# Two transformer layers on one core: queries, keys and attention outputs turned by DMA through DRAM instead of on TensorE, and layer 0's raw scores in blocks of 32 queries

## The reference

```python
# layer 0: 16 query heads and 4 key/value heads of 16 channels, rotary embedding, window of +-64 tokens
q, k = rope(x @ wq), rope(x @ wk); v = x @ wv
att = softmax(where(|i - j| <= 64, q k^T * 16 ** -0.5 + sink, -inf)); x = ln(x + (att @ v) @ wo)
x = ln(x + qmatmul(silu(qmatmul(x, w_gate)) * qmatmul(x, w_up), w_down))      # int8 weights, 1024 wide
# layer 1: 16 heads, causal, bias; then top 2 of 16 experts and a shared one
q, k, v = split(x @ w_qkv.T + b_qkv); q, k = rope(q), rope(k)
x = ln(x + (softmax(causal(q k^T / 4)) @ v) @ w_out.T + b_out)
x = ln(x + shared(x) + sum over the 2 chosen experts of weight * expert(x))
```

## Time and profile before

| | us |
|---|---|
| median of 3 runs | 926.04 (922.36 to 928.40) |
| the profiled execution | 922.61 |
| its span | 920.8 |
| PE busy, share | 772.8, 84% |
| DVE busy, share | 572.9, 62% |
| ACT busy, share | 456.1, 50% |
| POOL busy, share | 402.1, 44% |
| moved by DMA | 43.21 MB, 47 GB/s on average |

### The profile page before, as it was taken

One profiled execution on the slowest core, in us unless ns is written; L12 is line 12 of the kernel. 1 busy time (PEld: TensorE's weight loads), 2 busy tenths in 40 slices (PEclk: granted clock), 3 DMA queues, 4 the chain that ended last, 5 costly groups with the idle time before them and its releaser, 6 DMA issues.

```text
span 920.8 us, 15561 instructions
## 1 busy us (share of the span) xinstructions
PE 772.8 (84%) x5309; PEld 612.3 (66%) x5309; DVE 572.9 (62%) x1421; ACT 456.1 (50%) x990; POOL 402.1 (44%) x698
## 2 busy tenths in 40 slices
PE   5668888888878699977989999999978688899955
PEld 3567776766656577866756667766745566789845
DVE  4677776666523445457666677687741558699923
ACT  2226654555544344344455566667644243467503
POOL 4457655544455355566132234227155260145521
PEclk8879997999969899999699999999996589799978
DMA  8700000000000000000000000001045520245452
GB/s 227 178 1 1 2 2 1 1 2 2 2 1 1 0 1 1 1 1 1 2 1 1 2 2 1 3 1 48 1 165 186 122 91 9 81 139 156 138 207 92
DMA packets 26724, 43.21 MB, mean 47 GB/s; under 512 B 5972, under 2 KB 20054, under 8 KB 25784
## 3 DMA queue, kind: packets, MB, share of 16 engines
q0 software_dynamic: 6688, 23.30, 8.2%
q1 hardware_dynamic: 17248, 16.19, 6.3%
q10 hardware_dynamic: 2712, 2.73, 0.9%
HBM read 20.31 MB, written 14.60 MB: 38 GB/s over the span
## 4 chain that ended last, share of the span: by engine, by line
PE 65%; DVE 15%; POOL 8%; ACT 4%; issue 4%; DMA 2%; ACTq 0%; DVEq 0%; SPq 0%; POOLq 0%
PE ps L1726 9%; PE ps L1862 7%; PE ps L1880 7%; PE ps L1849 7%; PE ps L2287 4%; PE ps L2010 4%; DVE negmax L1310 3%; PE ps L1755 3%; PE ps L2027 3%; PE ps L2304 2%; PE ps L1842 2%; POOL fT L752 2%; PE ps L1764 2%; PE ps L2200 2%; PE ps L1845 2%
## 5 line engine op out<-in xcount | busy, mean ns | idle before, releaser
L1310 DVE TENSOR_REDUCE negmax<-ps 128x2 fp32r<-128x512 f32 (+4 forms) x304 | 189.6, 631 | 128.8 <-PE ps L1849 124.1
L941 ACT ACTIVATE prob<-ps 128x448 f32<-128x448 f32 (+2 forms) x320 | 168.8, 532 | 184.2 <-PE ps L1862 182.3
L1862 PE MATMUL ps<-qT,kT 128*128 128x256 f32 (+4 forms) x512 | 138.1, 337 | 42.9 <-DVE kT L1302 24.1
L1849 PE MATMUL ps<-kT,qT 128*128 128x256 f32 (+4 forms) x512 | 163.5, 389 | 0.0
L1862 PEld LDWEIGHTS ps<-qT,kT 128*128 128x128 f32 x512 | 87.8, 201 | 64.5 <-issue 51.3
L705 POOL TENSOR_SCALAR_AFFINE_SELECT prob<-prob 128x512 f32<-128x512 f32 (+1 forms) x192 | 115.8, 629 | 0.0
L1849 PEld LDWEIGHTS ps<-kT,qT 128*128 128x128 f32 x512 | 101.2, 212 | 2.6
L700 POOL TENSOR_TENSOR carry_p<-neg_half 128x1 f32<-128x1 f32 x80 | 16.7, 208 | 177.5 <-ACT prob L941 177.4
L1880 PE MATMUL ps<-prob,v_aug 128*32 128x256 f32 (+4 forms) x1024 | 84.8, 444 | 3.2 <-POOL prob L705 3.2
L836 POOL DMA_INDIRECT token_y<-ys_sb,y_row x47 | 45.0, 958 | 75.9 <-DVE ys_sb L1680 75.3
L1726 PE MATMUL ps<-wqkv_s,xh 128*128 128x384 f32 (+2 forms) x288 | 62.3, 354 | 10.1 <-DVE xh L1239 10.0
(11 more groups left out here) (237 smaller groups left out, 1673.0 us busy)
## 6 DMA issues: line engine op xcount, KB each, us to landing
xs_sb<-slot_x SPq DMA_DIRECT2D x47, 129.0 KB, 2.1
w_sb<-in_w POOLq DMA_DIRECT2D x4, 1408.0 KB, 12.0
w_sb<-in_w POOLq DMA_DIRECT2D x4, 704.0 KB, 9.6
x_all<-in_x SPq DMA_DIRECT2D x4, 512.0 KB, 9.4
slot_x<-zeros SPq DMA_DIRECT2D x1, 2048.0 KB, 22.6
w_sb<-token_y SPq DMA_DIRECT2D x2, 1024.0 KB, 10.4
w_sb<-token_y ACTq DMA_DIRECT2D x2, 1024.0 KB, 11.4
out<-y_all SPq DMA_DIRECT2D x4, 512.0 KB, 2.8
```

What stands on the lines that cost most here:

```text
L941: act.activation(prob[l][:, part % PROB_BUFS, i % GH, 0:cols], ps[:, 2 + n % 2, 0:cols], ACT.Exp, scale=SCALE).then_inc(exped[l].sem, 1)
L1310: dve.tensor_reduce(out=negmax[:, g % 2, t, j * mh:(j + 1) * mh], in_=ps[:, k % 2, 0:mh * n].rearrange("p (h n) -> p h n", n=n), axis=AX.X ...
L1849: ins = pe.matmul(dst[:, jj, :], qT[l][g % RING][:, h // 2, t * P:(t + 1) * P], kT[l][g % RING][:, h if l == 1 else h % 2, k0:k0 + n], sta ...
L1862: ins = pe.matmul(ps[:, 2 + item % 2, col:col + n], kT[l][g % RING][:, h if l == 1 else h % 2, kt * P:(kt + 1) * P], qT[l][g % RING][:, h ...
```

## The change

- **Queries and keys.** The projection is now made with the weights at rest and 512 tokens moving (`block_of`, L1901), so that it comes out transposed: 3 blocks for a batch in layer 0, 4 in layer 1 (there the values stay apart, `v_product1`). ACT copies a block to `raw_sb`, SP swaps the halves of each rotary pair by DMA (`swap`), POOL multiplies with the cosines, DVE with the sines and adds (`rope`), ACT and POOL make the high and the low part. SP writes both to DRAM (`write`) and reads them back for each group, already stacked as 48 rows for a head (`read`). `turn_q`, `turn_k`, the stacks and the copies of `qT` and `kT` are gone.
- **Attention outputs.** `oT` is written to DRAM and read back as numerators and denominators (`o_write`, `o_read_in`). For every two groups, in slot 4 of each odd step from 5 on, DVE takes the reciprocal of 512 columns and multiplies 512 (`divide`), then subtracts the high part (`o_low`). `o_transposes`, `o_turn` and the division of 16 columns are gone; the output products come one step later.
- **Raw scores of layer 0.** They go by blocks of 32 queries with 96, 128 or 160 keys. The four heads of the group lie beside each other on four column groups of PE, the operands are read as plain float32, and a group has 6 items, of 8, 8, 12, 12, 12 and 12 matmuls; four column groups of 32 are how `pv_part` too is laid out, before and after. The maxima are spread by one DVE operation and turned by one matmul.
- **Order.** In layer 1 the blocks of one batch instead of two are made in the feed-forward stage. Zeros for `slot_x`, 2 MB, are written after layer 0's steps instead of at the start; the later weights and inputs, 2.3 MB, stand behind the first group's read; the experts' first weights come at step 12 instead of 15, the shared ones after the scores.

What SP issues is now an ordered stream in which each entry waits for its own data, and all behind it wait with it.

```diff
-            def turn_q(l, g, n, bank):
-                pe.wait_ge(*q_lo[l].ge(g + 1))
-                for t in range(NT):
-                    ins = pe.matmul(ps[:, bank, t * P:(t + 1) * P],
-                                    q_st[l][g % Q_STACKS[l]][:, t, 2 * n:2 * n + 2, :].rearrange("p h s -> p (h s)"), ident_r[:],
-                                    start=True, stop=True)
-                ins.then_inc(q_tr[l].sem, 1)
...
+            def block_of(l, n, bank):
+                b, k = divmod(n, N_KINDS[l])
+                c0 = BLOCK_COLS[l][KINDS[l][k]]
+                pe.wait_ge(*xh_lo[l].ge(NT // 2 * (b + 1)))
+                for i, (a, w_part) in enumerate(EXACT):
+                    for k in range(KC):
+                        ins = pe.matmul(ps[:, bank, :], wqkv_s[l][:, w_part, k, c0:c0 + P], xh[:, a, k, :],
+                                        start=(i + k == 0), stop=(i == 2 and k == KC - 1))
+                ins.then_inc(blk[l].sem, 1)
...
+            def rope(l, n):
...
+                sines = rot[0:rows, 1, :] if rows == P else rot_k[0:rows, :]
+                dve.tensor_tensor(out=swap_sb[0:rows, n % 2, :], in0=swap_sb[0:rows, n % 2, :], in1=sines,
+                                  op=ALU.mult).then_inc(sined[l].sem, 1)
+                dve.wait_ge(*sined[l].ge(n + 1))
+                dve.wait_ge(*cosd[l].ge(n + 1))
+                dve.tensor_tensor(out=rope_sb[0:rows, n % 2, :], in0=rope_sb[0:rows, n % 2, :], in1=swap_sb[0:rows, n % 2, :],
+                                  op=ALU.add).then_inc(roped[l].sem, 1)
...
+            def write(l, n):
+                b, k = divmod(n, N_KINDS[l])
+                kind, rows = KINDS[l][k], rows_of(l, n)
+                m = 0 if kind == "kv" else int(kind[1])
+                dst, hi_at, lo_at = (q_dram, slice(0, 2), 2) if kind[0] == "q" else (k_dram, slice(0, 3, 2), 1)
+                sp.wait_ge(*hi_put[l].ge(n + 1))
+                sp.dma_start(dst[l][b, m, hi_at, :, :].rearrange("r p t -> p r t"),
+                             hi_sb[0:rows, n % 2, :].bitcast(F32).unsqueeze(1).to_broadcast([rows, 2, T])
+                             ).then_inc(stack_put[n % 2][l].sem, 16)
+                sp.wait_ge(*lo_put[l].ge(n + 1))
+                sp.dma_start(dst[l][b, m, lo_at, :, :], lo_sb[0:rows, n % 2, :].bitcast(F32)
+                             ).then_inc(stack_put[n % 2][l].sem, 16)
...
+            def read(l, g):
...
+                    q_rows = q_dram[0][b, gg // 2].rearrange("r (a l d j) t -> l (r a) d (j t)", a=2, l=2, d=HALF)
+                    k_rows = k_dram[0][b, 0].rearrange("r (a d h) t -> h (r a) d t", a=2, d=HALF)
+                    sp.dma_start(qT0[r][0:STACKED, :, :].bitcast(F32), q_rows[gg % 2]).then_inc(stacked[r][0].sem, 16)
+                    sp.dma_start(kT0[r][0:STACKED, :].bitcast(F32), k_rows[gg]).then_inc(stacked[r][0].sem, 16)
...
+                q_rows, k_rows = [d[1][b, gg // 2].rearrange("r (a l d s n) t -> l s (r a) d (n t)", a=2, l=2, d=HALF, s=2)[gg % 2]
+                                  for d in (q_dram, k_dram)]
+                for a in (0, 1):
+                    at = slice(a * STACK, a * STACK + STACKED)
+                    sp.dma_start(qT1[r][at, :, :].bitcast(F32), q_rows[a]).then_inc(stacked[r][1].sem, 16)
+                    sp.dma_start(kT1[r][at, 2 * a:2 * a + 2, :].bitcast(F32), k_rows[a]).then_inc(stacked[r][1].sem, 16)
...
+            def o_read_in(l, g):
+                c, at = g // 2, slice(g % 2 * STACK, (g % 2 + 1) * STACK)
+                rows = o_dram[l, g].rearrange("(j s d) t -> s j d t", s=2, d=HD)
+                sp.wait_ge(*o_written[g % 2][l].ge(16 * (g // 2 + 1)))
...
+                sp.dma_start(o_pack[l][at, c % 2, :], rows[0]).then_inc(o_read[c % 2][l].sem, 16)
+                sp.dma_start(den[l][at, :], rows[1]).then_inc(o_read[c % 2][l].sem, 16)
...
+            def stream(l):
+                for s in range(STEPS_OF_ATTENTION):
+                    blocks, before = blocks_of(l, s), blocks_of(l, s - 1)
+                    late = [n for i, n in blocks if i >= 5]
+                    if s + 1 < ALL_G:
+                        read(l, s + 1)
+                    if s >= 4:
+                        o_read_in(l, s - 4)
+                    if l == 1 and blocks:
+                        swap(l, blocks[0][1])
+                    if 1 <= s <= ALL_G:
+                        send_shift(l, s - 1)
+                    if l == 0 and blocks and not late:
+                        swap(l, blocks[0][1])
+                    for i, n in before:
+                        write(l, n)
+                    if l == 1 and blocks:
+                        swap(l, blocks[1][1])
+                    if s >= 3:
+                        o_write(l, s - 3)
+                    for n in late:
+                        swap(l, n)
+                o_read_in(l, ALL_G - 2)
+                o_write(l, ALL_G - 1)
+                o_read_in(l, ALL_G - 1)
...
-            def o_transposes(l, g):
-                pe.wait_ge(*oT_out[l].ge(g + 1))
-                if g >= 1:
-                    pe.wait_ge(*o_put[l].ge(g))
-                pe.wait_ge(*sh_out[l].ge(min(g + 3, ALL_G)))
-                for t in range(NT):
-                    ins = pe.transpose(ps[:, 5, t * P:(t + 1) * P], oT[:, t * P:(t + 1) * P], ident[:])
-                ins.then_inc(o_tr[l].sem, 1)
...
+            def divide(l, c):
+                dve.wait_ge(*o_read[c % 2][l].ge(64 * (c // 2 + 1)))
+                dve.reciprocal(den[l][:], den[l][:]).then_inc(inverted[l].sem, 1)
+                dve.wait_ge(*inverted[l].ge(c + 1))
+                dve.tensor_tensor(out=o_pack[l][:, c % 2, :], in0=o_pack[l][:, c % 2, :], in1=den[l][:],
+                                  op=ALU.mult).then_inc(divided[l].sem, 1)
...
+BLOCK_ITEMS = ((0, 15), (1, 14), (2, 3, 4), (5, 6, 7), (8, 9, 10), (11, 12, 13))
...
-                    pe.matmul(dst, ident_b[:], band[:, m0:m0 + n].unsqueeze(1).to_broadcast([P, mh, n]),
...
+                    for k, u in enumerate(us):
+                        k0 = block_keys(u)[0]
+                        for j in range(GH):
+                            ins = pe.matmul(dst[QB * j:QB * (j + 1), k * n:(k + 1) * n], qT0[r][0:RAW_ROWS[0], j, u * QB:(u + 1) * QB].bitcast(F32),
+                                            kT0[r][0:RAW_ROWS[0], k0:k0 + n].bitcast(F32), start=False, stop=True, skip_group_check=True)
...
-                for jj in range(mh):
-                    h = j * mh + jj
-                    ins = pe.matmul(dst[:, jj, :], qT[l][g % RING][:, h // 2, t * P:(t + 1) * P],
-                                    kT[l][g % RING][:, h if l == 1 else h % 2, k0:k0 + n],
-                                    start=False, stop=True, skip_group_check=True)
```

More of the change, by code:

```diff
@@ L506, in _ @@
+            for n in range(N_KINDS[0]):
+                swap(0, n)
+                if n >= 1:
+                    write(0, n - 1)
+            read(0, 0)
+            write(0, 2)
             for i in range(1, 4):
@@ L1448, in _ @@
-                if s >= 3:
-                    normalise(0, s - 3)
-            normalise(0, ALL_G - 1)
+                    if i == 1:
+                        for at, n in before:
+                            if at == 5:
+                                rope(0, n)
+                    if i in (2, 4) and b is not None:
+                        head_low(0, b * NT + i - 2, 8 - i // 2)
+                    if i == 4 and chunk_at(s) is not None:
+                        divide(0, chunk_at(s))
+                    if c is not None and i == 5 + c % 2:
+                        o_low(0, c)
@@ L1711, in keep_clock @@
                 for _ in range(n):
[L1712 to L1717 removed]
+                    pe.matmul(ps[:, 5, :].rearrange("p (a n) -> p a n", a=NT), ident_b[:],
+                              ident_b[:].unsqueeze(1).to_broadcast([P, NT, P]), start=True, stop=True)
```

1542 lines of the change are left out of this document (785 added, 757 removed).

## The result

The changed kernel takes 971.16 us (median of 4 runs, 961.65 to 973.05) where the one before takes 927.22 (922.36 to 929.12): the ratio is 1.046, with a 95% interval of 1.038 to 1.054. It is slower by 44 us, where 44 us less were forecast.

A forecast was written before the change was run, and what follows sets the result against it. PE was taken to bound the kernel, by its work and its waits. Start 0, layer 0 -15, its end +2, feed-forward -12, layer 1 -25, end +6 sum to -44 from 922.6, with 3.4 for the median 882 us; range 853 to 928.

The forecast's parts named there:

- the term for the traffic: Layer 1's steps: outputs read behind the operands land just before the division needs them; +3 us for steps with more traffic.
- The division waits for its data: Rival, chance 0.20: reads move in proportion to their rows, outputs land 2.2 us or more late in six steps; +20, 902.
- The round trips become the step: Rival, chance 0.12: DRAM traffic sets layer 1's step, 17 us and more, with half of 21 for experts' weights; 943.
- Layer 0, -15 forecast: Layer 0's attention: +2 for PE's work, -21 for waits on kT copies, +4 for the division.
- four slots or 5 us later, which hides it: Layer 0: PE needs the blocked maximum only then, so the division is hidden except where two norms follow; +4 us.
- The upper end of this term, +28: Layer 0's worst case: raw items at 7.9 us a step and all waits returned.
- Layer 1, -25 forecast: Layer 1's attention: PE's work, projections, waits and division give -28, traffic adds 3; range -44 to -4.
- -44 + 7 - 4: Layer 1: -44 for PE work that leaves the steps, +7 for projections, -4 for half of the 8.6 us of waits.
- The term of +13 for the reciprocal: Layer 1: PE waits 2.1 to 2.3 us for a maximum queued behind the division, six times in steps 5 to 15.
- Feed-forward and the end of layer 0, -10 forecast: Feed-forward -12 from cheaper projections and turns that leave; end of layer 0 +2 for the last output through DRAM.
- Start, 0 forecast: Start-up: three added DMA trips and the second read's delay set against removed work and 2 MB of zeros; -5 to +8.
- End, +6 forecast: End of layer 1: last output's trip through DRAM and division, +5, and shared weights loaded later, +1; range +3 to +12.

The follow-up runs named there:

- e1: The changed kernel with SP asking for the attention outputs before the next group's operands: 925.89 us, 1.003 of the kernel before.
- e3: The changed kernel with layer 1's weight columns reordered so that the 48 rows of a read lie evenly spaced in DRAM: 944.68 us, ratio 1.024.
- e4: The changed kernel with the experts' first weights asked for at step 15 instead of 12: 963.63 us, ratio 1.042.
- e2: The changed kernel with the high and low parts of the divided outputs made in later slots of steps 7, 11 and 15: 966.38 us, ratio 1.045.
- the pieces: The reciprocal of 512 columns cut into four of 128 in successive slots; on e1 and e2 together 904.74 us, ratio 0.979; also part of e10.
- e6: e1 with the reciprocal replaced by a copy of 512 columns, so the output isn't the reference's: 891.67 us, ratio 0.964.
- e7: e1 with the early loads of weights and inputs, 2.3 MB, behind the third group's reads instead of the first's: 928.02 us, ratio 1.002.
- e5: e1 with the experts' second weights, 2.8 MB, asked for after the last division: 915.79 us, ratio 0.989.
- e10: e1 and e2 with the reciprocal in four pieces, plus e3's even rows and e5's late second weights: 894.77 us, ratio 0.968.

## Why the prediction was wrong

**The step that failed is the term for the traffic, +3 for outputs that "just" arrive in time.** "1.05 MB at 432 GB/s are 2.4 us, at 263 they are 4.0, and with landing 4.5 to 6.1, against 5 x 1.2 = 6.0 us until slot 4 ends. That just holds": it did not. The reads moved at 114 GB/s at a DMA share of 0.35, and the outputs landed 9.8 us after their issue and 13.4 after the first read's. The difference, 3.7 us, are SP's issues of six DMAs one after the other, for which the prediction had no term. The whole was worth 45 us by e1, 30 of them in layer 1. The two rates came from stretches with transfers of other shapes, over 128 rows, at DMA shares of 0.93 and 1.13, and e3 shows that the order of the rows decides: the same bytes move at 174 to 197 GB/s.

By the rule of the Trainium skill that the prediction cites (DMA: Bandwidth & Descriptors, Why a DMA increments its semaphore by 16 and not by 1) the outputs were estimated to land some 9 us into the step, 3 too late. That pointed the right way, and the trace shows 13.4.

The lateness comes on top of the division. From the end of the third maximum DVE serves nobody for 6.5 + 4.05 us and then takes 0.5 for the next one, of which the two raw items ahead cover some 3: PE waits 8.25 us, where the sum had 2.1 to 2.3. And one of the waits, 24.5 us, is for the most part not the operand reads but the experts' 5.6 MB (e4, 15 us of layer 1), which the prediction left out of its sum and had in the rival of the round trips alone.

**Which rival it was.** "The division waits for its data" named the mechanism and gave 902; it was right in place and in sign of the term, and its price of 20 us was too small by a factor of more than two (45 by e1), for the reasons above and because of layer 0, where it counted nothing and e1 gains 14. "The round trips become the step" gave 943, nearest in time, and that is luck, since its mechanism was not there: in after PE's waits for operands behind the start are 1.0 us. Only its term for the experts' weights, half of 21 us, has something in e4.

**Layer 0, -15 forecast, +7.** The raw items (+2.3 a step, measured 5.9 against 5.8) and the turns that left were right. The first four steps, which have no division, lasted 10.4, 10.5, 11.2 and 13.0 us against 13.8, 12.2, 12.1 and 12.2 before; the steps with one lasted up to 19.0. The step that failed is "four slots or 5 us later, which hides it": DVE's queue had the slack, but ACT's copy of the divided outputs stands in slot 4 or 5 ahead of exponentials and waits for DVE, so that PE's two score banks ran dry instead (e2's waits); 14 of the 22 us between forecast and measurement are the late outputs (e1). With the outputs first, layer 0's 15 steps are 191.8 us, 7 less than before, and with the pieces 186.4, 13 less. The upper end of this term, +28, does not come out of its own numbers: 16 x (7.9 - 3.5 - 2.2) are 35 with all waits returned, and the division makes it 39. Nothing hangs on it here.

**Layer 1, -25 forecast, +34.** PE's work was right in size: the first four steps, with no division, lasted 12.4, 13.6, 11.5 and 14.7 us, 13.1 on average, where the terms without the division (-44 + 7 - 4 from 16 steps of 16.0) leave 13.4. The term of +13 for the reciprocal was a stall of 2.1 to 2.3 us in each of six steps; its size can't be told apart from the wait in after, but e6 puts the reciprocal at 34 us in the whole kernel where the prediction had 13 + 4 + 3: 17.6 in layer 1 for its 13, 6.7 in layer 0 for its 4, 2.5 behind for its 3, and 8.3 between the layers, for which it had none.

**Feed-forward and the end of layer 0, -10 forecast, -17.6.** Right in sign; the stretch also holds the last steps of layer 0 and the first of layer 1, so that the gain can't be put to the projections alone.

**Start, 0 forecast, +8.5.** The chain of three trips ended at 35.6 us (before 32.2), which was taken as even, and the second group's operands, behind 2.3 MB, came at 58.0. The prediction had both and set them off against the 2 MB of zeros that left the start, and no run shows that these had delayed anybody. e7 takes 8.4 us off the start by the loads alone.

**End, +6 forecast, +16.** The trips were priced by a transfer alone, 2.1 us; with 3.9 MB of weights asked for around them they took 6.0 and 15.4 us. e5 gives 10 back by 2.8 MB of them alone.

What stays open: what the pieces are worth without e2, and how much of PE's lower granted clock (0.864 over the span against 0.907) is in these numbers. It fell in the long waits (0.65 in 642 to 681), and no run here holds it apart from them; 0.880 in e1 and 0.897 in e10 are still below the kernel before.

## What to carry to other kernels

Price a transfer by its own shape: bytes over the bandwidth of another one, however measured, can mislead by a factor of two or more (263 to 432 GB/s taken, 114 measured), and the order of the rows in DRAM alone moved it to 174 and more. Count the issues too where one engine makes them all: six took 3.7 us. Where a consumer stands at a fixed place in an engine's order, ask for its data first in the queue, ahead of what is wanted a step later, and count what stands behind the waiting instruction on every engine that passes the wait on. A long operation on an engine that serves a two-deep ring can be worth cutting to pieces, even if that makes its sum longer: here four of 0.93 us for one of 3.35.
